# Adding each expert tile's gated result to the output rows, in place of a mixing stage at the end

## What is computed

```python
x = x + attention(layernorm(x), adj)                 # 4096 x 256
xn = layernorm(x)
probs = softmax(xn @ W_router)                       # 8 experts
topk_p, topk_i = top_k(probs, 2); topk_p /= topk_p.sum()
for e in range(8):                                   # C = 256, H = 1024
    h = relu(xn @ W1[e] + b1[e])
    y = h @ W2[e] + b2[e]
    out += combine[:, e:e+1] * y                     # combine is 0 for tokens that don't use e
x = x + out
```

## Time and profile before

| what | us |
|---|---|
| median of 3 runs | 1078.3 (1078.14 to 1080.27) |
| the profiled execution's own time | 1078.58 |
| its span, first to last instruction | 1077.0 |
| mean granted TensorE clock | 0.860 of full speed |
| busy: PE / DVE / ACT / POOL | 801.0 / 691.7 / 466.4 / 446.9 |

### The profile page before, as it was taken

One profiled execution on the slowest core, in us unless ns is written; L12 is line 12 of the kernel. 1 busy time (PEld: TensorE's weight loads), 2 busy tenths in 40 slices (PEclk: granted clock), 3 DMA queues, 4 the chain that ended last, 5 costly groups with the idle time before them and its releaser, 6 DMA issues.

```text
span 1077.0 us, 23781 instructions
## 1 busy us (share of the span) xinstructions
PE 801.0 (74%) x6721; PEld 730.2 (68%) x6722; DVE 691.7 (64%) x1989; ACT 466.4 (43%) x1309; POOL 446.9 (41%) x440
## 2 busy tenths in 40 slices
PE   1588887879887863234615999999999999999900
PEld 1477786868786752234514988899888898889900
DVE  9887878887888754287264555565655645554455
ACT  2333534343444342132403565555555556566600
POOL 5177777777777751266772000000000000007455
PEclk8578999999899986655556999999999999999955
DMA  9614313133031110042356324142414232124346
GB/s 265 221 45 109 100 30 100 51 80 103 23 101 25 26 34 2 3 154 83 133 184 206 108 88 137 60 140 82 138 58 136 97 103 82 58 73 138 110 134 187
DMA packets 108881, 107.94 MB, mean 100 GB/s; under 512 B 18275, under 2 KB 98100, under 8 KB 108720
## 3 DMA queue, kind: packets, MB, share of 16 engines
q1 hardware_dynamic: 85680, 65.32, 19.9%
q0 software_dynamic: 23168, 42.22, 13.3%
HBM read 93.10 MB, written 40.37 MB: 124 GB/s over the span
## 4 chain that ended last, share of the span: by engine, by line
PE 40%; issue 22%; POOL 19%; DVE 12%; DMA 4%; ACT 1%; POOLq 1%; DVEq 1%; ACTq 0%; SPq 0%
POOL nbr L435 14%; PE psE L1191 10%; PE psH L1180 6%; PE psH L1181 6%; PE psH L1182 6%; PE psE L1193 5%; POOL expert_in L482 4%; DMA xg<-expert_out,gpos 2%; PE psY L1029 1%; PE psX L1167 1%; DMA nbr<-xn_rows,idx 1%; PE psL L1143 1%; DVE stats L554 1%; PE psXT L1134 1%; DVE w_parts L907 1%
## 5 line engine op out<-in xcount | busy, mean ns | idle before, releaser
L435 POOL DMA_INDIRECT nbr<-xn_rows,idx x256 | 269.9, 1054 | 110.4 <-issue 107.1
L909 DVE TENSOR_TENSOR h_lo<-z_all,h_hi 128x256 fp32r<-128x256 f32 x296 | 125.3, 423 | 155.7 <-ACT h_hi L1366 155.7
L1365 ACT ACTIVATE z_all<-psH,b1e 128x256 f32<-128x256 f32 x296 | 141.6, 478 | 174.0 <-PE psH L1182 173.9
L1191 PE MATMUL psE<-w_parts,h_hi 128*128 128x512 f32 x552 | 210.1, 407 | 1.3 <-DVE h_lo L909 1.2
L1180 PE MATMUL psH<-x_hi,w_hi 128*128 128x256 f32 (+1 forms) x592 | 167.7, 283 | 12.8 <-issue 8.3
L1181 PE MATMUL psH<-x_lo,w_hi 128*128 128x256 f32 (+1 forms) x592 | 168.1, 284 | 0.0
L1182 PE MATMUL psH<-x_hi,w_lo 128*128 128x256 f32 (+1 forms) x592 | 167.8, 283 | 0.0
L579 DVE MAX8 best<-codes 128x8 f16<-128x1024 f32 x128 | 149.1, 1220 | 16.3 <-PE codes L991 11.4
L1193 PE MATMUL psE<-w_parts,h_lo 128*128 128x256 f32 x552 | 155.3, 281 | 0.0
L1366 ACT ACTIVATE h_hi<-psH,b1e 128x256 fp32r<-128x256 f32 x296 | 140.4, 474 | 0.0
L1029 PEld LDWEIGHTS psY<-diag,nbr 128*128 128x128 f32 x1024 | 133.5, 210 | 7.2 <-issue 4.8
(11 more groups left out here) (260 smaller groups left out, 1113.8 us busy)
## 6 DMA issues: line engine op xcount, KB each, us to landing
adj_raw<-in_adj SPq DMA_DIRECT2D x8, 2048.0 KB, 10.2
w_raw<-in_L_ffn_W POOLq DMA_DIRECT2D x16, 1024.0 KB, 6.3
x_in<-expert_in SPq DMA_DIRECT2D x38, 256.0 KB, 2.7
expert_out<-y_out SPq DMA_DIRECT2D x37, 256.0 KB
early_out<-y_out SPq DMA_DIRECT2D x32, 256.0 KB, 2.4
nbr<-xn_rows,idx POOLq DMA_INDIRECT x264, 2.1
x_all<-in_x SPq DMA_DIRECT2D x4, 1024.0 KB, 9.0
xn_rows<-row_all SPq DMA_DIRECT2D x4, 1024.0 KB, 4.5
```

The lines of the kernel that those rows point to most:

```text
L435: pool.indirect_dma_start(nbr[:, u, k, :], None, xn_rows, bass.IndirectOffsetOnAxis(ap=idx[:, u, k:k + 1], axis=0), bounds_check=N - 1, oo ...
L909: dve.tensor_tensor(h_lo[:, hc, :], h_f[:, hc, :], h_hi[:, hc, :].bitcast(F32), ALU.subtract).then_inc(hl_ready, 1)
L1191: pe.matmul(psE[:, q, :], h_hi[:, hc, m], w2_parts[:, b, hc].rearrange("p s c -> p (s c)"), start=(hc == 0), stop=False)
L1365: act.activation(h_f[:, hc, :], psH[:, hc % 4, 0:T], ACT.Relu, bias=b1e[:, b, hc:hc + 1])
```

## The change

Each row of `expert_in` grows from 256 to 260 values: behind the token's values stand its number (`TOK`), the number of its first expert plus an offset that a DVE instruction gives it (`FIRST`), and the difference of its two logits (`LESS`, two columns). Rows that pad a tile carry the token number 4096, which is out of bounds for `out` and skipped there.

In routing SP stores `x_all` to `out` after the attention result is in (four stores of 1 MB), and takes over all weight loads. DVE writes the extra columns, and no longer makes the result positions, the tile rows and the gate weights. In an expert tile DVE copies the marks (token number and first expert) out of `x_in`, ACT takes the exponential of `LESS`, and DVE works out the gate with four small instructions ahead of the tile's first `h_lo`. POOL gathers the 256 output rows of the tile's tokens into `acc` (two indirect DMAs). After `y_out` DVE computes `y_out * gate + acc` (two instructions), and POOL scatters the result back to `out` (two indirect DMAs). Within an expert the next tile's gather doesn't wait for the scatters' landing (a token occurs once in an expert); for the first tile of the next expert it does. DVE's `y_part` now waits until the scatters of the tile before have landed (`y_free`) instead of until the store has (`yo_stored`). The result tables, their zeroing, `place`, `mix` and `fetch` are gone.

The core of the diff:

```diff
 def load_tile(n, row):            # SP
     wait_alone(sp, x_ps, n + 1)
+    wait_alone(sp, marks_ready, n + 1)
+    wait_alone(sp, less_ready, n + 1)
     sp.dma_start(x_in[:], expert_in[bass.ds(row, T), :]...)
...
+def rows_of_tile(n, after):       # POOL
+    wait_alone(pool, marks_ready, n + 2)
+    pool.tensor_copy(tok_next[:], marks[:, :, 0]).then_inc(tok_taken, 1)
+    wait_alone(pool, tok_taken, n + 2)
+    if after:
+        wait_alone(pool, y_scattered, n * (TS * 16))
+    for q in range(TS):
+        pool.indirect_dma_start(acc[:, q, :], None, out, ...tok_next[:, q:q + 1]...).then_inc(acc_ready, 16)
+def add_tile(done):
+    wait_alone(pool, acc_ready, done * (TS * 16))
+    pool.tensor_copy(tok_now[:], tok_next[:]).then_inc(tok_kept, 1)
+    wait_alone(pool, tok_kept, done)
+    for q in range(TS):
+        wait_alone(pool, y_ready, done * TS + q + 1)
+        pool.indirect_dma_start(out, ...tok_now[:, q:q + 1]..., y_out[:, q, :], None, ...).then_inc(y_scattered, 16)
+def added(done):
+    wait_alone(pool, y_scattered, done * (TS * 16))
+    pool.sem_inc(y_free, 1)
...
+# per expert: for i in 1..count-1: add_tile, rows_of_tile(False), added;
+# then add_tile, added, and rows_of_tile(True) for the next expert's first tile
...
+def gate_of(n, e):                # DVE, ahead of a tile's h_lo
+    wait_alone(dve, marks_ready, n + 2)
+    dve.wait_ge(less_ready, n + 2)
+    dve.scalar_tensor_tensor(gate[:, 0], marks[:, :, 1].bitcast(F32), iota_f[:, 0, bass.ds(e, 1)], less_exp[:],
+                             ALU.is_equal, ALU.max).then_inc(gate_step, 1)
+    dve.tensor_scalar(gate[:, 1], less_exp[:], 1.0, None, ALU.add).then_inc(gate_step, 1)
+    wait_alone(dve, gate_step, n * 4 + 2)
+    dve.reciprocal(gate[:, 2], gate[:, 1]).then_inc(gate_step, 1)
+    wait_alone(dve, gate_step, n * 4 + 3)
+    dve.tensor_tensor(gate[:, 3], gate[:, 0], gate[:, 2], ALU.mult).then_inc(gate_step, 1)
...
     rest_of_x(n + 1)              # now also copies the marks, after a wait for tok_taken
-    wait_alone(dve, yo_stored, n * 16 + 16)
+    wait_alone(dve, y_free, n + 1)
     ...                           # y_part, y_out as before
+    wait_alone(dve, acc_ready, n * (TS * 16) + TS * 16)
+    wait_alone(dve, gate_step, n * 4 + 4)
+    for q in range(TS):
+        wait_alone(dve, yo_ready, n * TS + q + 1 + TS)
+        dve.scalar_tensor_tensor(y_out[:, q, :], y_out[:, q, :], gate[:, 3, q:q + 1], acc[:, q, :],
+                                 ALU.mult, ALU.add).then_inc(y_ready, 1)
...
 act.copy(x_hi..., psX[:]).then_inc(xh_ready, 1)      # ACT, part_of_x
+act.activation(less_exp[:], x_in[:, :, LESS], ACT.Exp).then_inc(less_ready, 1)
...
 # DVE, route (each block of 1024 tokens)
+dve.tensor_copy(xg[:, b, :, TOK].bitcast(I32), tok_i[:, bass.ds(q * QT, QT)])
+dve.tensor_scalar(xg[:, b, :, FIRST], e12[:], float(E), None, ALU.add)
-step(dve.tensor_tensor(d_all[:, bass.ds(q * QT, QT)], m12[:, 1], m12[:, 0], ALU.subtract))
+dve.tensor_tensor(xg[:, b, :, LESS:CX], ..., ALU.subtract).then_inc(extras_ready, 1)
-step(dve.tensor_copy(posf[:, :, bass.ds(q * QT, QT)], posq[:]))
```

More of the change, by code:

```diff
@@ L208, in attention_and_experts @@
         y_part = sb("y_part", [P, TS, C], F32, ffn)
-        e_rows = xg[:, 0, 0:GT, :]
-        lower = [a for rows in (z_all[:, NT // 2:NT, :], w1_raw[:].rearrange("p k (j c) -> p (k j) c", c=C), w2_raw[:])
-                 for a in (rows[:, t, :] for t in range(rows.shape[1]))]
+        acc = sb("acc", [P, TS, C], F32, ffn)
+        marks = sb("marks", [P, TS, 2], U32, ffn)
+        tok_now = sb("tok_now", [P, TS], U32, ffn)
+        tok_next = sb("tok_next", [P, TS], U32, ffn)
+        less_exp = sb("less_exp", [P, TS], F32, ffn)
+        gate = sb("gate", [P, 4, TS], F32, ffn)
         ffnp = ExitStack()
@@ L486, in _ @@
                 scatter(i * 2 + 1, 1)
-            with pool.Fori(2, E) as e:
-                for m in range(2):
-                    wait_alone(pool, w_split, (e - 1) * SPLITS + (m + 1) * (SPLITS // 2))
-                    load_weights(e, m)
-            total = pool.value_load(plan[0:1, 3, 0:1], min_val=E, max_val=MAX_TILES)
-            early = pool.value_load(plan[0:1, 1, E - 1:E], min_val=E - 1, max_val=MAX_TILES - 1)
-            rest = pool.value_load(plan[0:1, 4, 0:1], min_val=1, max_val=2 * MAX_TILES + 2)
@@ new lines, in added, with tiles @@
+            def added(done):
+                wait_alone(pool, y_scattered, done * (TS * 16))
+                pool.sem_inc(y_free, 1)
+            def tiles(e, following):
+                count = pool.value_load(plan[0:1, 0, bass.ds(e, 1)], min_val=1, max_val=N // T)
+                before = pool.value_load(plan[0:1, 1, bass.ds(e, 1)], min_val=0, max_val=MAX_TILES)
+                with pool.If(count > 1):
+                    with pool.Fori(1, count) as i:
+                        add_tile(before + i)
+                        rows_of_tile(before + i, False)
+                        added(before + i)
+                add_tile(before + count)
+                added(before + count)
+                if following:
+                    rows_of_tile(before + count, True)
@@ L513, in _ @@
+            rows_of_tile(0, False)
+            with pool.Fori(0, E - 1) as e:
+                tiles(e, True)
+            tiles(E - 1, False)
         @block.vector
@@ L883, in _ @@
-            for c in range(2):
-                link(dve.tensor_tensor(swap[:, 2], swap[:, 1], gates[:, c], ALU.mult))
-                link(dve.tensor_tensor(swap[:, 3], swap[:, 0], gates[:, 1 - c], ALU.mult))
-                link(dve.tensor_tensor(mix_by[:, c], swap[:, 2], swap[:, 3], ALU.add))
+            dve.tensor_copy(plan[:, 5], plan_f[0:1, 8]).then_inc(planned, 1)
+            dve.memset(acc[:], 0.0).then_inc(acc_clear, 1)
             dve.sem_inc(yo_ready, TS)
-            dve.sem_inc(yo_stored, 16)
+            dve.sem_inc(y_free, 1)
@@ L891, in _ @@
+            dve.sem_inc(y_ready, TS)
+            dve.sem_inc(marks_ready, 1)
+            dve.sem_inc(tok_taken, 1)
             dve.sem_inc(hl_ready, HC)
@@ L1331, in route @@
                     if u < QT:
-                        act.activation(xg[:, b, u, :], tile(x_all, q * QT + u), ACT.Identity, bias=rs2[:, b, 4, u:u + 1],
+                        act.activation(xg[:, b, u, 0:C], tile(x_all, q * QT + u), ACT.Identity, bias=rs2[:, b, 4, u:u + 1],
                                        scale=rs2[:, b, 0, u:u + 1]).then_inc(xg_ready, 1)
@@ L1344, in _ @@
             act.wait_ge(planned, 1)
-            act.activation(gates[:, 1], d_all[:], ACT.Exp).then_inc(d_exp, 1)
             act.sem_inc(hf_ready, 4)
+            act.sem_inc(less_ready, 1)
             def part_of_x(n):
```

204 lines of the change are left out of this document (70 added, 134 removed).

## The result

The changed kernel takes 1110.6 us (median of 3 runs, 1109.26 to 1112.72) where the kernel before takes 1078.3: the ratio is 1.030, with a 95% interval of 1.027 to 1.033. It is slower, where the forecast was 1043.5. The profiled execution has a span of 1108.64 us against 1076.98, 31.7 more.

The account below looks back on a forecast made before the run. PE was taken to set the expert stage (busy 432 of 449 us). From 1078.6 us, the tail's -47.8, routing's +0.6 and the tiles' +12.1 gave 1043.5; range 1032 to 1063, with 0.50 for 1037 to 1050.

Parts of the forecast that it names:

- The tail: End of the kernel: mixing stage of 52.6 us replaced by two multiply-adds and two scatters, 47.8 us saved.
- POOL's own last wait: End of the tail: from the last scatter's landing at 1028.9 to the end of the span at 1029.2.
- Routing: Before the first tile: two small DVE instructions per block and start-up work, +0.6 us (0.3 to 5.5).
- The slack: Tile ends within experts: 1.5 us of DVE work against 1.02 of slack, 10.6 us lost over 22 plain ends.
- rival (b): Tile ends: dear register waits or gate column reads on DVE, 2.1 us added and beyond, 29 lost: 1060; chance 0.14.
- Half tiles: Five ends before half tiles, counted among the 22 plain ends: +2.4 us.
- Ends between experts: Seven ends where DVE is idle for 1.48 us ahead of the cast: nothing lost.
- The range: Whole kernel: 1032 to 1063 us, taking in (a), (b) and (c), with under 2 in 10 outside.
- POOL's chain (d): Each tile: chain from multiply-add to `y_free` on POOL becomes the limit, 89 us lost at 11.5 us: 1120; chance 0.06.
- POOL's DMAs are held up by DVE at each border: Tile borders, by the skill's figure: four DMAs late by some 10 us each time, sum about 50 us higher.

Follow-up runs that it names:

- e5b_fma_only: The kernel before plus only two dummy multiply-adds on DVE behind `y_out`, written to an unused buffer, without the gate: 1085.2 us.
- e5_dummy: The kernel before plus DVE's new work as a dummy: the gate ahead of each tile and two multiply-adds behind `y_out`: 1121.7 us.
- e3_unroll: The changed kernel with DVE's loop over pairs of experts written out in full, so that it never jumps back: 1101.5 us.
- e7_small: The changed kernel with the gate in mid-tile and folded into the additions of the sums, and DVE's loop over single experts: 1053.5 us.
- e6_wide: The kernel before with expert rows of 260 values instead of 256 in routing's buffers, DRAM and the first load, nothing else: 1077.1 us.
- e2_no_dve: The changed kernel without DVE's gate and its two multiply-adds, so the output isn't the layer's; POOL's gathers and scatters stay: 1036.7 us.

## Why the prediction was wrong

Two steps failed. The first is that PE loses only what goes beyond the slack of a plain end: half tiles lost 22.2 us instead of 2.4, most of it through the clock. The second is that nothing is lost between experts: it was 24.3 us, 15.2 of them at the two ends where DVE's loop jumps back. With these two as predicted and all else as measured, the sum would be -12.4 us and the kernel faster than before. The steps in order:

**The tail** was right to 3.6 us (44.2 instead of 47.8 saved). The landing of the last scatter was right (2.1 us, 2.4 taken). The term that was mis-sized is the end behind it, "POOL's own last wait" of 0.3 us: it is 3.4 us, 3.0 of them POOL's DRAIN. In the kernel before, POOL's DRAIN (6.8 us) was over before SP's last store had landed, and so cost nothing. Most of the rest is POOL's reaction, 0.9 us from the end of the first multiply-add to the first scatter instead of 0.3 to 0.5.

**Routing** was +4.9 instead of +0.6, inside the bound of 5.5 that the step gave, but not for its reason. The last landing took 2.58 us, 0.2 more, not 4.7. What the step left out are SP's two reads of the plan, which the change moved behind the wait for the scatters (1.8 us); the way from the first scatter to block 2 grew by 1.4 where 0.5 was put; and 1.3 is the spread of the first scatter's start.

**The slack** was right: e5b_fma_only shows that 0.7 us disappear in it. What was put in was 1.86 us, not 1.5: I had priced the gate at 0.20 a dependent step, from the routing chain, and it took 0.31. PE's restart behind a late `h_lo` took 0.40, not 0.14. By the prediction's own formula, 1.86 - 1.02 + 0.26 = 1.10 us, and the trace has +0.99 to +1.23 (18.8 us over 17 ends); for e5_dummy it gives 1.58 - 1.02 + 0.26 = 0.82, and 0.86 was measured. That is rival (b) in mechanism, at 1.86 of its 2.1 us. With this alone the sum would have been wrong by some 14 us, and still inside the range.

**Half tiles** were counted as plain ends. Each pays about 1.3 us where the clock stays, 6.7 us in all, and the fall to 1.2 GHz took another 15.4. The sentence that PE's loss is what goes beyond the slack took each matmul's duration as fixed. The trace of the kernel before spoke against that, and I didn't look: the mean of 0.99 in the earlier trace rows isn't 1.00. PE waits 0.7 to 1.6 us at each end between experts there too, ahead of the expert's first matmul, and just behind the longest of these waits, 1.63 us (to 699.01), the clock is at 1.2 GHz for 3.4 us (the table by stage):

```profile
699.80:703.20 3.40, 3.40 (x18) 3.40 (x17) 2.29 (x6) 2.27 (x6) 0.00 (x0) 0.50 0.55 176
```

**Ends between experts** were put at 0, on 1.48 us of idle time ahead of the cast. Two things were wrong in that. The idle time was read as slack in full, but most of it stays: behind the multiply-adds DVE stands 1.26 us again, put down to issue. And a tile with splits is set by DVE, which has no gap from the cast to `y_part`, so each microsecond shows in full. In the runs such ends lost 0.2 to 1.0 us with the multiply-adds alone and 1.0 to 2.6 in the changed kernel.

**The holes at the jumps**, 7.2 and 8.0 us of loss, were in no step and in no rival. I counted the gate's and the multiply-adds' time, and not that all code of a tile stands several times in the loop's body. e3_unroll (gone without the jump) and e7_small (gone with the short body) show between them that it takes a jump over a long body.

**The range.** It was 1032 to 1063 with 0.06 for slower. The only rival on the slower side was POOL's chain (d), which didn't happen: in the changed kernel `y_part` never waited for `y_free`. The rivals were priced one at a time with a single size of loss for each end; none changed the clock or the rhythm of the tiles that DVE sets. That POOL's DMAs are held up by DVE at each border, by the figure of the Trainium skill ("SBUF — State Buffer", "SBUF: two separate sides"), isn't so here. The gathers and scatters of the tiles by line (ns: min, median, max) in the changed kernel:

```profile
L483 POOL DMA_INDIRECT acc<-out,tok_next x74: 1009/1049/1303, 585.6 to 1092.1; - x74
...
L492 POOL DMA_INDIRECT out<-y_out,tok_now x74: 986/1032/1262, 602.0 to 1103.1; - x74
```

What was held up beside DVE's splits were tensor copies on POOL (4 us twice in the changed kernel), and none of these was waited for.

## What to carry to other kernels

Find the engine that sets each kind of tile, and its slack there, before placing work: here 0.7 us disappeared at a plain end, and the same work showed in full in tiles that the other engine already set. Put small dependent chains where their result isn't awaited (moving four tiny instructions gave 48 us). Where PE will wait, read what the granted clock does after such a wait, since the loss can be several times the wait; and count what an edit adds to the body of a loop, not only to its time. Look also at what an edit moves behind the last wait of a chain: two register reads of SP there cost 1.8 us.

## What the runs showed of the hardware

- A loop on DVE whose body grew paid 5 to 8 us at two jumps back, with three packets of the instruction queue in that time; with half the body none. In the kernel before, DVE stands there only 0.5 us longer than at the other ends within the loop. At which length it begins isn't measured.
- The granted clock fell to 0.50 behind PE waits of 1.10 to 1.24 us in four of five half tiles of the changed kernel, and after waits of 0.8 to 1.2 us in its plain full tiles it never did. The length of the wait doesn't decide it: in e3_unroll five half tiles had waits of 1.08 us and the clock fell in three, in e5_dummy, with waits of 0.89 to 0.94, it fell in one of five. It also fell in tiles with splits, behind waits of 2.46 and 1.80 us in the changed kernel and 1.63 in the kernel before. What else it needs the runs don't tell.
- PE started 0.39 to 0.40 us after the end of an `h_lo` for which it had waited 0.6 us or more, and 0.15 after one for which it had waited 0.2 to 0.5.
- With rows of 1040 bytes plain tiles were 0.12 us shorter (11.69 instead of 11.81, e6_wide, one trace), about 1% in the pace of the matmuls. The cause wasn't looked for.
- A POOL copy of 128x2 values, 0.2 us otherwise, took 4.0 and 3.9 us in the changed kernel, 6.9 us in e3_unroll, and 7.1, 7.6 and 7.5 us in e2_no_dve, all in tiles in which DVE split weights.
- POOL's DRAIN at the end of the program took 3.0 us in the changed kernel, though its last scatter had landed before it began.
